# Probabilities of the first three tiles in fp32: turned on TensorE, with one fp32 value product a head

## The reference, cut to what matters

```
xn   = layernorm(x)
q    = rms_norm(xn @ q_w.T + q_b) * norm_q;   k = rms_norm(ctx @ k_img_w.T + k_img_b) * norm_k
v    = ctx @ v_img_w.T + v_img_b
p    = softmax(q k^T / sqrt(32))              # 16 heads, 128 x 128 each
x1   = x + tanh(g_xattn) * ((p v) @ o_w.T + o_b)
h    = relu(layernorm(x1) @ w1.T) ** 2        # w1, w2: ternary weights, scaled in groups of 64
out  = x1 + tanh(g_ffn) * (rms_norm(h) @ w2.T)
```

## Time and profile before

| | us |
|---|---|
| median of three runs | 930.18 (928.06 to 931.1) |
| the profiled execution | 929.98 |
| its span in the profile | 928.2 |
| TensorE (PE) busy | 887.7 (96%) |
| ACT busy | 787.7 (85%) |
| DVE busy | 711.0 (77%) |
| GpSimd (POOL) busy | 556.4 (60%) |

### The profile page before, as it was taken

How to read it: one execution, slowest core, us unless ns; L and a number is a source line. 1 busy time by engine, 2 the same in 40 slices (tenths; PEclk the granted TensorE clock), 3 DMA queues, 4 the chain that set the end, 5 groups by cost and what they waited for, 6 DMA issues and landing times. The chain is left out here.

```text
span 928.2 us, 22544 instructions
## 1 busy us (share of the span) xinstructions
PE 887.7 (96%) x7632; PEld 534.1 (58%) x7729; DVE 711.0 (77%) x1528; ACT 787.7 (85%) x1582; POOL 556.4 (60%) x618
## 2 busy tenths in 40 slices
PE   5999889999999999999999999999999999999998
PEld 2455555655556566555565666555655665556664
DVE  5889999878788787878888787878887787877301
ACT  6788999888988888888988888889888888898673
POOL 2322165676667666666676666766666567657674
PEclk9999999999999999999999999999999999999999
DMA  8597775466566665656676556676666555745200
GB/s 320 156 196 181 136 195 126 80 131 125 120 129 120 132 112 110 128 121 115 126 121 131 121 110 124 116 134 106 137 117 114 113 122 118 126 93 102 69 24 35
DMA packets 319747, 115.79 MB, mean 125 GB/s; under 512 B 305168, under 2 KB 305168, under 8 KB 318096
## 3 DMA queue, kind: packets, MB, share of 16 engines
q1 hardware_dynamic: 319632, 114.34, 59.9%
HBM read 30.67 MB, written 8.39 MB: 42 GB/s over the span
## 5 line engine op out<-in xcount | busy, mean ns | idle before, releaser
L2195 POOL TENSOR_TENSOR hh_sum<-hh_sum,hh_sb 128x512 f32<-128x512 f32 x112 | 143.9, 1285 | 126.3 <-ACT hh_sb L1061 125.8
L570 PE MATMUL up_pair<-ft,w 128*128 128x256 f16 x960 | 214.6, 272 | 1.7 <-ACT h_sb L1034 0.9
L571 PE MATMUL up_pair<-ft,w 128*128 128x256 f16 x960 | 214.5, 272 | 0.0
L586 PE MATMUL mix_pair<-w,big 128*128 128x512 bf16 x480 | 181.9, 379 | 7.2 <-issue 2.4
L2185 POOL TENSOR_TENSOR big<-h_sb,big 128x512 f16<-128x512 f32 x128 | 154.7, 1209 | 16.6 <-ACT h_sb L1043 8.9
L585 PE MATMUL mix_pair<-w,big 128*128 128x512 bf16 x397 | 150.5, 379 | 0.1
L1034 ACT ACTIVATE h_sb<-up_pair,relu_scale 128x512 f32<-128x512 f32 x120 | 81.7, 681 | 60.7 <-PE up_pair L571 60.5
L570 PEld LDWEIGHTS up_pair<-ft,w 128*128 128x128 bf16 x960 | 93.8, 98 | 20.4 <-DMA ft<-x_rows 2.5
L571 PEld LDWEIGHTS up_pair<-ft,w 128*128 128x128 bf16 x960 | 93.8, 98 | 16.5
L2140 POOL TENSOR_TENSOR ln_rstd<-ln_in,minus_half 128x1 f32<-128x1 f32 x64 | 44.4, 693 | 96.8 <-issue 90.4
L1109 ACT ACTIVATE score_pair<-score_pair,exp_bias,exp_scale 128x128 f32<-128x128 f32 x232 | 85.0, 431 | 1.1 <-DVE exp_bias L1651 0.9
(11 more groups left out here) (246 smaller groups left out, 2327.9 us busy)
## 6 DMA issues: line engine op xcount, KB each, us to landing
x_sb<-in_x SPq DMA_DIRECT2D x32, 256.0 KB, 3.3
ctx_sb<-in_ctx_t SPq DMA_DIRECT2D x32, 256.0 KB, 3.1
out<-out_sb SPq DMA_DIRECT2D x32, 256.0 KB, 2.4
big<-in_w_fc_t SPq DMA_DIRECT2D x4, 1024.0 KB, 5.4
big<-in_w_proj_t SPq DMA_DIRECT2D x4, 1024.0 KB, 6.0
pt<-p_rows SPq DMA_TRANSPOSE x128, 2.8
big<-in_wq_t SPq DMA_DIRECT2D x1, 1024.0 KB, 7.5
big<-in_wk_t SPq DMA_DIRECT2D x1, 1024.0 KB, 9.6
```

The costliest lines, as they stand in the source:

```text
L570: nc.tensor.matmul(dst[:, half], w, ft[i][:, c, :], start=(c == 0), stop=False)
L571: last = nc.tensor.matmul(dst[:, half], w, ft[i][:, C + c, :], start=False, stop=(c == C - 1))
L586: last = nc.tensor.matmul(dst[:, :], ht_lo[i][:, row], w2[:, m, :], start=False, stop=(m == M - 1))
L2195: nc.gpsimd.tensor_tensor(hh_sum[:, :], hh_sum[:, :], hh_sb[f % 2][:, :], ALU.add).then_inc(hsum_ready, 1)
```

## The change

For tiles 0 to 2 (`FULL = 3`) the probabilities are not halved. `exps` writes its fp32 result to SBUF, into the memory of `p_rows` read as fp32 (`p_full`). TensorE turns it, four 128x128 fp32 blocks a bank, back into the same PSUM bank (`turn`), and DVE copies it to `pt`, read as fp32 (`probs_turned`). `values` makes one fp32 matmul a head from it, with the values in fp32 in `v_full` (the memory of `v_both`); `v_lo_of` is left out for these tiles. The twelve `probs_hi`, `probs_lo` and `transpose_p` of tiles 0 to 2 go. `next_keys`, `next_queries`, `next_values` and the next `scores` wait for the copy instead of for `probs_lo`. The ones in `v_both` are written as fp32 first and once more, as fp16 halves, before tile 3 (`value_columns`).

The lists of all five engines are in another order up to tile 6, and the loop behind them is the same. The multiset of calls is otherwise kept: all ternary pieces, all 51 `warm` matmuls.

```diff
+        p_full = [rows[:, :, :].rearrange("p n k -> p (n k)").bitcast(F32) for rows in p_rows]
+        pt_full = [rows[:, :, :].rearrange("p n k -> p (n k)").bitcast(F32) for rows in pt]
+        v_full = v_both[:, :, :].rearrange("p h c -> p (h c)").bitcast(F32).rearrange("p (h c) -> p h c", c=HD + 1)
...
+            def turn(t, b):
+                pe.wait_ge(consts_ready, 5)
+                pe.wait_ge(exp_ready, 4 * t + b + 1)
+                for u in range(4):
+                    col = slice(u * P, (u + 1) * P)
+                    last = nc.tensor.transpose(score_ps[b][:, col], p_full[(4 * t + b) % PR][:, col], ident[:, :])
+                last.then_inc(turn_done, 1)
...
             def scores(t):
-                pe.wait_ge(vlo_ready, t + 1)
-                need(pe, plo_ready, 4 * t)
+                if t < FULL:
+                    pe.wait_ge(vhi_ready, t + 1)
+                else:
+                    pe.wait_ge(vlo_ready, t + 1 - FULL)
+                for b in range(4 if t > 0 else 0):
+                    probs_split(t - 1, b)
...
             def values(t):
                 for b in range(4):
-                    pe.wait_ge(pt_in[b], 16 * t + 16)
+                    if t < FULL:
+                        pe.wait_ge(turned_ready[b], t + 1)
+                    else:
+                        pe.wait_ge(pt_in[b], 16 * (t - FULL) + 16)
                     for u in range(4):
+                        if t < FULL:
+                            last = nc.tensor.matmul(dst, pt_full[b][:, q], v_full[:, h, :], start=True, stop=True)
+                            continue
                         nc.tensor.matmul(dst, pt[b][:, 0, q], v_hi[:, h, :], start=True, stop=False)
                         nc.tensor.matmul(dst, pt[b][:, 0, q], v_lo[:, h, :], start=False, stop=False)
                         last = nc.tensor.matmul(dst, pt[b][:, 1, q], v_hi[:, h, :], start=False, stop=True)
...
             def exps(t, b):
+                if t < FULL:
+                    need(act, turn_done, n - PR + 1)
+                    dst = p_full[n % PR]
+                else:
+                    dst = score_ps[b]
                 if t < EARLY:
-                    nc.scalar.activation(score_ps[b][:, :], score_ps[b][:, :], ACT.Exp, scale=exp_scale[:, :],
+                    nc.scalar.activation(dst[:, :], score_ps[b][:, :], ACT.Exp, scale=exp_scale[:, :],
                                          bias=log_scale[:, :]).then_inc(exp_ready, 1)
...
+            def probs_turned(t, b):
+                n = 4 * t + b
+                dve.wait_ge(turn_done, n + 1)
+                if b == 0:
+                    need(dve, alo_ready, t)
+                else:
+                    need(dve, pv_done, n - 3)
+                nc.vector.tensor_copy(pt_full[b], score_ps[b][:, :]).then_inc(turned_ready[b], 1)
...
+            spread_weight(0, up_b)
+            first_query()
             spread_weight(1, up_b)
-            first_query()
```

More of the change, by code:

```diff
@@ L857, in _ @@
             shift(0, 2)
+            turn(0, 0)
             shift(0, 3)
+            turn(0, 1)
+            turn(0, 2)
             next_keys(0)
             next_queries(0)
+            turn(0, 3)
+            values(0)
+            ternary_pair(1, 1)
             next_values(0)
-            values(0)
+            next_context(0)
+            ternary_pair(2, 1)
             warm(5, 1)
-            ternary_pair(2, 1)
-            next_context(0)
             warm(5, 1)
-            warm(4, 1)
             scores(1)
             ternary_pair(3, 1)
+            warm(4, 1)
             shift(1, 0)
@@ L886, in _ @@
             shift(2, 0)
+            shift(2, 1)
             ternary_pair(8)
-            shift(2, 1)
+            turn(2, 0)
             shift(2, 2)
+            shift(2, 3)
+            turn(2, 1)
+            turn(2, 2)
             next_keys(2)
-            shift(2, 3)
+            turn(2, 3)
+            ternary_pair(9)
             next_queries(2)
-            ternary_pair(9)
             spread_fc_top()
             next_values(2)
+            values(2)
+            next_context(2)
             ternary_pair(10)
-            values(2)
@@ L898, in _ @@
             warm(5, 3)
+            ternary_half(22)
+            ffn_up(0, 2, 0, up_ps, 1)
+            scores(3)
             warm(6, 3)
             warm(6, 3)
-            next_context(2)
-            ffn_up(0, 2, 0, up_ps, 1)
-            scores(3)
             ffn_up(0, 2, 1, up_ps, 1)
+            ternary_half(23)
             project_out(2)
-            ternary_half(22)
+            next_keys(3)
+            warm(4, 3)
+            ternary_half(24)
+            next_queries(3)
+            ternary_half(25)
@@ L907, in _ @@
             ffn_up(0, 2, 2, up_ps, 1)
-            next_keys(3)
-            ternary_half(23)
-            next_queries(3)
-            ternary_half(24)
+            ternary_half(26)
+            values(3)
             next_values(3)
-            warm(4, 3)
-            values(3)
-            ternary_half(25)
-            ternary_half(26)
+            ffn_up(0, 2, 3, up_ps, 1)
             next_context(3)
-            ffn_up(0, 2, 3, up_ps, 1)
+            warm(6, 4)
             ffn_up(0, 3, 0, up_ps, 1)
+            scores(4)
@@ L920, in _ @@
             ternary_half(27)
-            scores(4)
+            ffn_up(0, 3, 1, up_ps, 1)
+            project_out(3)
+            ffn_up(0, 3, 2, up_ps, 1)
+            warm(6, 4)
+            next_keys(4)
             ternary_half(28)
-            warm(6, 4)
-            warm(6, 4)
-            ffn_up(0, 3, 1, up_ps, 1)
+            next_queries(4)
+            ffn_up(0, 3, 3, up_ps, 1)
+            ternary_half(29)
             warm(4, 4)
-            project_out(3)
-            next_keys(4)
@@ L1356, in _ @@
+            halves(0, 2, 0)
+            ternary_abs(12)
             exps(3, 0)
@@ L1923, in _ @@
-            weight_lo(3)
-            probs_lo(0, 1)
-            k_out(1)
-            probs_lo(0, 2)
-            probs_lo(0, 3)
+            probs_turned(0, 1)
+            probs_turned(0, 2)
+            k_out(1)
+            q_out(1)
+            probs_turned(0, 3)
+            attention(0, 0)
+            attention(0, 1)
+            k_lo(1)
+            ternary_clip(0)
+            q_lo(1)
             ternary_mask(0)
-            q_out(1)
-            x_lo(2)
+            ternary_signed(0)
@@ L2013, in _ @@
+            normed_lo(1)
+            attention(2, 0)
+            attention(2, 1)
+            k_lo(3)
+            context_top(4)
+            q_lo(3)
+            context_scale(4, 1)
+            ternary_clip(10)
+            ternary_signed(8)
+            x_lo(4)
+            value_columns()
+            attention_lo(2)
+            ternary_half(22)
             v_lo_of(3)
-            ternary_mask(8)
-            ternary_signed(8)
-            context_top(4)
+            ternary_final(8)
             ternary_signed(9)
-            attention_lo(2)
@@ L2039, in _ @@
-            q_out(4)
-            next_context(5)
-            ternary_half(24)
-            k_lo(4)
-            attention(3, 0)
-            ternary_half(25)
-            attention(3, 1)
-            ternary_mask(12)
+            ternary_mask(11)
+            attention(3, 0)
+            ternary_signed(11)
+            attention(3, 1)
+            q_lo(4)
+            x_lo(5)
+            k_lo(4)
+            ternary_mask(12)
+            attention_lo(3)
+            ternary_final(10)
+            ternary_final(11)
```

626 lines of the change are left out of this document (303 added, 323 removed).

## The result

The changed kernel took 937.89 us (median of 5 runs, 935.76 to 938.98); the kernel before, in the same session, 928.27 us (5 runs, 927.78 to 931.10). The ratio is 1.0092, with a 95% interval of 1.0071 to 1.0114. The forecast of 932.4 us, which counted as no change, was wrong: the change costs 9.6 us (6.6 to 10.6 by the interval). That lies outside the forecast's own range (929 to 933) and just inside the wide one (926.5 to 938). In three later sessions the kernel before stood somewhat higher, at medians of 929.8 to 930.6 us, so 9.6 is more likely a little too much than too little.

What follows compares the result with a forecast made beforehand. TensorE (PE) was taken as the bound. Added work of 12.7 us, less 8.0 of waits and 2.3 at the start, gave +2.4 on 929.98, so 932.4 us; own range 929 to 933, 8 in 10 range 926.5 to 938.

Steps and rivals of the forecast that it cites:

- rival 3: Slots of tiles 0 to 2: turns bring a half-pace clock stretch in each, +10 us, 942; over 938 had chance 0.05.
- high price of turns: The 48 transposes at about 275 ns each: 13.2 us, 7.9 more than forecast, about 940 us; over 938 had chance 0.05.
- PE's added work, +12.7: Between scores(0) and scores(4), PE gets 5.3 us of turns and 7.4 us of longer value products; range 7.1 to 18.0.
- The waits that go, -8.0: Six slots before scores(6): of 11.6 us PE idle time, 8.0 go and 3.6 stay; ends 4 and 14.
- The start, -2.3: Up to scores(0): tile 0's query ahead of the second weight's spread brings scores(0) 2.3 us sooner; ends 0 and 4.
- The half pace at the start: Tile 0's query took 5.47 us against tile 0 key's 3.44, read as half pace though the clock reads 1.00.
- The copies at 0.68 us: Twelve DVE copies out of PSUM take 0.68 us each, like the low halves they replace; 0.42 would gain 3.1 us.
- The removed DMA turns: SP loses twelve turns of tiles 0 to 2, worth only the 1.1 us that PE waited for them.
- Rival 1: Longer value product delays next scores, 1.2 us wait in each of three tiles: +6.0, 936.2 us; 0.33 with smaller forms.
- Rival 2: Shorter way from exponentials to values lets turned work fill all idle time, 14 us: -3.6, 926.5 us; chance 0.19.

Runs made afterwards that it cites:

- fp16_in_after: after_c with each fp32 value product of tiles 0 to 2 replaced by three matmuls of constant 16-bit tiles, turns kept; 924.40 us.
- fp32_values_c: base_c with the 48 fp16 value matmuls of each of tiles 0 to 2 replaced by 16 fp32 ones on constant tiles; 929.49 us.
- quarter_c: after_c with one of four blocks turned per bank, so 36 of 48 transposes left out; 930.73 us.
- act_copies_c: after_c with the twelve copies of turned probabilities on ACT instead of DVE; 932.83 us.
- base_c: The kernel before with each DMA transpose replaced by a plain DMA to the same destination, nothing turned by them; 923.18 us.
- after_c: The changed kernel with each DMA transpose replaced by a plain DMA to the same destination, nothing turned by them; 932.61 us.
- start_c: base_c with the changed kernel's order up to scores(0), tile 0's v_lo kept, DVE's later work in the author's own order; 928.66 us.
- fp32_filler_c: fp32_values_c with 24 unused 16-bit matmuls of 248 columns, 8 a tile, among the fp32 value products; 929.28 us.

## Why the prediction was wrong

The step that failed is the clock. The prediction read a granted clock of 1.00 in all stretches, named its fall as rival 3, tied that to the transposes and gave it 0.05 together with the high price of turns. It came in every run of the changed kernel (mean clock 0.995 to 0.996 in all five, against 0.998 at worst in the kernel before), at 4.8 us in the profiled execution. That is half the 10 us named, because a fall lasted 3.4 us of time, in which 1.7 us of work took double, and not 3.4 us of work. The cause was misplaced too: it is the value products (fp16_in_after, fp32_values_c), not the turns (quarter_c). The rule quoted there from the Trainium skill ("TensorE: Matmul & The Clock Gate", "Part 4: PE-mode transpose") speaks of transposes alone. Here 48 of them beside fp16 value products left the clock at 1.00 in every slot, so they are not what a fall needs; whether they count for anything isn't shown.

Step by step:
- **PE's added work, +12.7:** measured 11.8 to 12.4. Turns 5.3 forecast, 5.6 found; value products +7.4 forecast, +6.2 to +6.8 found (0.109 us a record; the row with one column had 0.118). That 33 columns cost no more than one was right.
- **The waits that go, -8.0:** 5.4. This is the second term that was off, by 2.6 us. The slot of 3.83 us fell to 1.42, as argued, but those of 1.62 and 2.14 only to 1.36 and 1.66, and that of 1.12 rose to 1.30. The prediction worked from how full DVE and ACT are, and misread the waits: it names two groups, of 2.0 and 1.1 us, and says "nothing longer" of the rest. This one is longer than the second, and longer than any single wait of the two (the kernel before, 32.7 to 187 us):

```profile
PE mix_pair L523 <- DMA at<-at_rows: 1.5, 1, 1.5
```

  The slot of 3.83 us is made of this 1.50, of 1.10 for `out_sb` of DVE, 0.78 for `h_sb`, and 0.29 and 0.16 more. In the changed kernel it holds one wait, 1.42 for DVE's `out_sb` (L1655). The waits are for single results, and added PE time covers only those that it happens to stand ahead of. act_copies_c speaks for that, as it takes 2.4 us a slot off DVE and leaves PE's idle time where it was. Which chain each wait belongs to was read from the waits, not tested.
- **The start, -2.3:** 2.84, scores(0) at 29.88. How much of it is the order and how much the execution isn't clear: in the six kernels with plain DMAs and the whole new order scores(0) came at 29.6 to 31.0 us, against 32.3 in base_c. The removed v_lo is up to 0.6 of it: scores(0) waited 0.6 us for it in the kernel before and in base_c, and in the changed kernel it waited for nothing that the trace shows. The path itself was not shown apart.
- **The half pace at the start:** the prediction sets it against a clock that reads 1.00. Tile 0's query needs 3.44 us at full pace and took 5.47 from 14.34, so its first 2 x 2.03 = 4.1 us went at half pace, to 18.4. The trace's clock record has its first entry at 18.44, and the view prints 1.00 for what lies ahead of it. In the changed kernel the same sum gives 15.8 (5.26 us from 12.11), and the first entry stands at 15.77. So that 1.00 was no reading.
- **The copies at 0.68 us:** 0.680 to 0.688. The Trainium skill ("VectorE: DVE Perf Modes", "Why PSUM operands drop a tier") holds DVE to one element a cycle with fp32 in PSUM; the trace agrees.
- **The removed DMA turns:** no wait for turned probabilities is left in tiles 0 to 2, 1.1 us as said.
- **Rival 1:** its time, 936.2 (counted from the median of 930.18, where the forecast counts from 929.98), was the nearest of the rivals', but by luck. Its wait showed once, before scores(3), and not in each of three tiles: 0.4 us in the changed kernel, 1.2 in fp16_in_after. **Rival 2** fell: the turned work did not fill the hidden idle time. The wide range was called 8 in 10, but the chances given leave 0.19 below it and 0.05 above, 0.76 in it.

The sum as it came: +12.4 (at most) + 4.8 - 5.4 - 2.8 = +9.0, of 9.26 measured at scores(6); the 0.3 to 0.9 us left are in PE's busy time and not assigned. In the kernels with plain DMAs the same loss of 9.4 us parts into 1.2 (turns, copies, order), some 5.6 (the length of the value products, from 924.4 to the 930 that after_c's runs point to with no fall; the timelines give 5.4) and some 2.6 (falls, fewer in those runs). The last two are estimates, since no run of after_c was without a fall.

What stays open: why the same code is followed by a fall in one execution and not in another, where the single fall of the kernel before lies, and what the new start is worth alone.

## What to carry to other kernels

Before a short fp16 product on a loaded TensorE is turned into fp32 with few moving columns, price two things: the length of each record, here 0.11 to 0.12 us with 1 column and with 33 (with 33 the weight load was busy all the time), and a possible 3.4 us at half clock behind a row of 32 such records. Such a row looks fully busy in the trace, so look at the clock in stretches of a few us, and not at PE's share. When a forecast counts on waits being filled, name for each wait the single result it waits for; the mean load of the engines doesn't say.

## What the runs showed that I had not expected

- The granted clock falls to 0.50 behind 3.5 us of gapless fp32 products of 33 columns, with PE 100% busy and PE's weight load 100% busy (48 to 49 us above); the same fall began 1.6 us into a wait of PE of 3.8 us (start_c). One fall lasts 3.4 us, twice or four times that; each 3.4 us cost 1.2 to 1.8 us.
- It comes in some executions of the same kernel and not in others: fp32_values_c's times fall into two groups 3.6 us apart by it.
- With eight plain matmuls of 248 columns among the 32 records of a tile the clock stayed up in 12 of 12 runs (fp32_filler_c), without them in 5 of 10, and the eight lengthened the row by only 0.33 us.
